# Counting the chosen memory rows once, from one-hot rows summed on GpSimd, in place of once per token tile on TensorE

## The reference

```python
qp = jnp.einsum('bld,ed->ble', q, Wq)
scores = jnp.einsum('bld,bmd->blm', qp, kv)
idx = jnp.argmax(scores, axis=-1)
mem = jnp.take_along_axis(kv, idx[..., None], axis=1)
mkv = jnp.einsum('bld,ed->ble', mem, Wkv)
mk, mv = jnp.split(mkv, 2, axis=-1)
logits = jnp.einsum('bhld,bmd->bhlm', qh, mk) * scale
attn = jax.nn.softmax(logits, axis=-1)
out = jnp.einsum('bhlm,bmd->bhld', attn, mv)
```

## Time and profile before

| | |
|---|---|
| Time, median of 3 runs | 1332.48 us (1331.79 to 1332.91) |
| Span of the profiled execution | 1333.5 us, 1.0 us above that median; no other time is given for it |
| PE busy | 1184.3 us (89%) |
| DVE busy | 975.1 us (73%) |
| ACT busy | 624.8 us (47%) |
| POOL busy | 182.8 us (14%) |
| Lookup stage | about 625.6 to 750 us |

### The profile page before, as it was taken

One profiled execution on the slowest core, in us unless ns is written; L12 is line 12 of the kernel. 1 busy time (PEld: TensorE's weight loads), 2 busy tenths in 40 slices (PEclk: granted clock), 3 DMA queues, 4 the chain that ended last, 5 costly groups with the idle time before them and its releaser, 6 DMA issues. The chain is left out here.

```text
span 1333.5 us, 18190 instructions
## 1 busy us (share of the span) xinstructions
PE 1184.3 (89%) x6745; PEld 633.7 (48%) x6745; DVE 975.1 (73%) x2195; ACT 624.8 (47%) x838; POOL 182.8 (14%) x165
## 2 busy tenths in 40 slices
PE   7994899999999999974999389999986799999997
PEld 3541223333333333243788112333334489899997
DVE  3564999898899988046799489999918466767675
ACT  1220245756756666741443015666653334444442
POOL 2223111021021100143000430500004000000000
PEclk9995799999999999986999559999987899999999
DMA  7215167920000000030110593200011000000000
GB/s 257 72 59 113 25 69 80 113 27 1 2 1 1 1 1 2 1 133 27 48 48 1 57 99 42 89 2 2 1 45 61 1 1 1 17 1 16 1 17 17
DMA packets 44760, 51.72 MB, mean 39 GB/s; under 512 B 7322, under 2 KB 40090, under 8 KB 44666
## 3 DMA queue, kind: packets, MB, share of 16 engines
q1 hardware_dynamic: 44666, 50.50, 19.7%
HBM read 38.36 MB, written 11.53 MB: 37 GB/s over the span
## 5 line engine op out<-in xcount | busy, mean ns | idle before, releaser
L572 ACT ACTIVATE self_probs<-self_scores 128x1024 f32<-128x1024 f32 (+3 forms) x320 | 273.3, 894 | 197.2 <-PE self_scores L526 195.9
L600 DVE TENSOR_REDUCE self_piece_max<-self_max 128x1 f32<-128x512 f32 x384 | 249.7, 685 | 22.9 <-PE self_max L511 21.4
L511 PE MATMUL self_max<-stack_k,stack_q 96*128 96x512 bf16 (+3 forms) x640 | 209.1, 367 | 21.2 <-DVE self_piece_max L600 9.0
L600 DVE TENSOR_REDUCE cross_piece_max<-cross_max 128x1 f32<-128x512 f32 x256 | 160.7, 683 | 25.6 <-PE cross_max L511 25.0
L572 ACT ACTIVATE cross_probs<-cross_scores 128x1024 f32<-128x1024 f32 x128 | 124.6, 1021 | 109.3 <-PE cross_scores L526 109.3
L526 PE MATMUL self_scores<-stack_q,stack_k 98*128 98x512 bf16 (+3 forms) x640 | 170.5, 350 | 4.3 <-DMA stack_q<-self_shift 3.0
L511 PEld LDWEIGHTS self_max<-stack_k,stack_q 96*128 96x128 bf16 x640 | 61.7, 97 | 201.8 <-DVE self_piece_max L600 102.5
L537 PE MATMUL self_out<-self_probs,V 128*17 128x512 f32 (+3 forms) x1280 | 148.8, 537 | 2.4 <-ACT self_probs L572 2.1
L596 DVE CUSTOM_DVE_ANT_0 self_junk<-self_max,causal_sb 128x128 bf16<-128x128 f32 (+3 forms) x256 | 120.8, 484 | 21.0 <-PE self_max L511 19.5
L1259 ACT ACTIVATE o_tok<-ph 128x512 f32<-128x512 f32 x96 | 57.5, 599 | 143.6 <-PE ph L92 137.4
L92 PE MATMUL py<-w_first,hid_first 128*128 128x256 f32 x384 | 108.7, 283 | 5.8 <-DVE x_sb L1321 5.8
(11 more groups left out here) (207 smaller groups left out, 1799.1 us busy)
## 6 DMA issues: line engine op xcount, KB each, us to landing
stack_q<-qparts SPq DMA_DIRECT2D x96, 64.0 KB, 8.9
stackx<-xparts SPq DMA_DIRECT2D x24, 256.0 KB, 11.1
stack_k<-kparts SPq DMA_DIRECT2D x18, 256.0 KB, 14.3
qparts<-parts SPq DMA_DIRECT2D x8, 384.0 KB, 2.5
kparts<-parts SPq DMA_DIRECT2D x8, 384.0 KB, 2.5
xparts<-xparts_sb SPq DMA_DIRECT2D x8, 384.0 KB, 2.8
cross_raw<-in_w SPq DMA_DIRECT2D x4, 768.0 KB, 4.4
n_raw<-in_w SPq DMA_DIRECT2D x6, 512.0 KB, 4.2
```

Source lines behind the costliest of these rows:

```text
L511: mm = nc.tensor.matmul(slot[:, 0:pc["w"]], pc["lhsT"], pc["rhs"], start=True, stop=True)
L572: nc.scalar.activation(probs[:, i % 3, 2 * pair:2 * pair + 2, st["off"]:C], ps[:, 2 * pair:2 * pair + 2, st["off"]:C], ACT.Exp, scale=SCAL ...
L600: ins = nc.vector.tensor_reduce(to, slot[:, 0:pc["w"]], AX.X, ALU.max)
```

## The change

The 13 matmuls for each tile go, and with them a matmul that cleared `pc`. In their place GpSimd adds each tile's one-hot rows to a sum `hits`, in place, 16 additions over 1601 elements of bf16. After the last of them PE multiplies `hits` with the column of ones, 13 matmuls once. `chosen` has 1601 columns for each buffer where it had 1664, and `hits` has 1664 and is cleared at the stage's start in place of `chosen`.

```diff
-                    chosen = sb(inner, "chosen", [P, 2, MP], BF16)
+                    chosen = sb(inner, "chosen", [P, 2, M], BF16)
+                    hits = sb(inner, "hits", [P, MP], BF16)
...
-                            nc.gpsimd.memset(chosen[:], 0.0).then_inc(set2, 1)
+                            nc.gpsimd.memset(hits[:], 0.0).then_inc(set2, 1)
...
+                            pool.wait_ge(set2, 3)
+                            for n in range(NT):
+                                pool.wait_ge(chosen_ready, n + 1)
+                                if n:
+                                    pool.wait_ge(counted, n)
+                                nc.gpsimd.tensor_tensor(hits[:, 0:M], hits[:, 0:M], chosen[:, n % 2], ALU.add).then_inc(counted, 1)
...
-                            def tally(n):
-
-                                pe.wait_ge(chosen_ready, n + 1)
-                                for t in range(MT):
-                                    mm = nc.tensor.matmul(pc[:, t:t + 1], chosen[:, n % 2, t * P:(t + 1) * P], ones_b[:, 0:1],
-                                                          start=False, stop=(n == NT - 1 and t == MT - 1), skip_group_check=True)
-                                mm.then_inc(counted, 1)
-
                             pe.wait_ge(set2, 6)
-                            nc.tensor.matmul(pc[:, 0:MT], zeros_b[:, 0:P], zeros_b[:, 0:MT], start=True, stop=False, skip_group_check=True)
...
-                                if n >= 2:
-                                    tally(n - 2)
-                            tally(NT - 2)
-                            tally(NT - 1)
+                            pe.wait_ge(counted, NT)
+                            for t in range(MT):
+                                mm = nc.tensor.matmul(pc[:, t:t + 1], hits[:, t * P:(t + 1) * P], ones_b[:, 0:1], start=True, stop=True)
+                            mm.then_inc(counted, 1)
...
-                                nc.vector.tensor_scalar(chosen[:, n % 2, 0:M], iota_sb[:], place_f[:, n % 2], None,
+                                nc.vector.tensor_scalar(chosen[:, n % 2], iota_sb[:], place_f[:, n % 2], None,
                                                         ALU.is_equal).then_inc(chosen_ready, 1)
...
-                            dve.wait_ge(counted, NT)
+                            dve.wait_ge(counted, NT + 1)
```

## The result

| | before | changed |
|---|---|---|
| Median of 20 runs each | 1333.05 us (1331.79 to 1335.63) | 1335.51 us (1332.48 to 1338.00) |
| Ratio, 95% interval | | 1.0015 (1.0009 to 1.0021) |
| Span of the profiled execution | 1333.5 us | 1335.6 us |
| First MAX8 to the counts read (L1086, now L1085) | 94.17 us | 95.08 us |
| First MAX8 to the next stage's first DMA | 104.77 us | 106.18 us |

The account below looks back on a forecast made before the run. PE was taken to bound the later tiles by a little, DVE right behind; 3.06 us gained in the loop, 3.94 lost at its end, the rest nothing: 1332.5 + 0.9 = 1333.4 us, range 1331.5 to 1338.0 for 8 in 10.

Parts of the forecast that it names:

- The loop gain: Tile loop without 14 tallies of 0.34 us on PE: MAX8 of tile 15 at 729.73, 3.06 us earlier.
- The halved clearing: GpSimd's clearing at the stage's start, 1664 for 3328 elements: nothing gained, since a DMA wait covers it.
- The addition A: GpSimd's addition of 1601 elements per tile: 3.06 us, with 1.6, 3.59 and 4.59 kept as ends.
- The hold: A DVE one-hot row stands still while a GpSimd addition runs and ends 0.80 us after it.
- The threshold: Inside the loop, additions start to cost through held one-hot rows from A = 3.85 us.
- The counts: DVE's read of the counts after the loop: 740.33 against 739.45 before, 0.9 us slower.
- the step on the clock: PE idles from about 730 to 740; should its clock rise later than before, a few tenths are lost.
- PE's lead: Tiles 2, 3, 4, 7 and 8 are set by DVE, or DVE and ACT; their tallies are hidden.
- The odd one-hot rows: Rival: rows in the second `chosen` buffer take 1.83 us for 1.06; 5.5 us slower, 1338.0; chance 8%.
- The additions did not outlast a tile: Rival that they do: at A = 4.59 pace 5.44, 12 us slower, 1344.6; 3.85 to 4.59 costs 3 to 12; 8%.
- A DVE that isn't held: Rival, loop end: without hold 0.1 us slower; or, with additions of 1.6 us, 1.4 faster, 1331.1; chance 14%.
- The loop did not gain more: Rival that it does: tiles set by DVE come out earlier, counts 1.7 us earlier with it all; 3%.

Follow-up runs that it names:

- the repeat of before: The kernel before run once more, nothing changed: ratio 0.9996 (0.9985 to 1.0007) to the kernel before.
- the filled kernel: Changed kernel plus three matmuls of zeros on PE behind the scores of tiles 3 and 7: ratio 1.0022 (1.0012 to 1.0032) to the kernel before.
- the repeat of the changed kernel: The changed kernel run once more, nothing altered: ratio 1.0010 (0.9997 to 1.0023) to the kernel before.

## Why the prediction was right, and where it was short

**The loop gain** was right in its size and its places: 3.06 us forecast, 3.15 measured. That 4.8 us of PE work gave only that was DVE's doing, at tiles 5, 6, 9 and 10, as worked out. Leaving the additions out changed nothing (91.00 against 91.01), so it is the tallies' gain alone. The halved clearing gave nothing, as forecast: it took 1.49 us for 2.88, and GpSimd's wait for the DMA behind it grew from 1.10 to 2.48.

**The addition A** was taken as 3.06 us from the row of 1602 elements. It is 3.25 at a multiple of 4 bytes and 2.94 off it; the two that matter are 3.21 and 2.93, in sum 6.14 for the 6.12 of the forecast. The trace of before also had 1024 elements at 2.37 us, where the forecast's line of 0.27 us and 1.75 ns an element gives 2.06; with the 1536 at 3.45 that made two rows against the line. That the sum fits so well is luck, since the forecast knew nothing of the two lengths: with both buffers aligned it was 3.21 + 3.20 = 6.41, and the counts came 0.28 us later. Still, the row nearest in size was the right choice; the 3.59 scaled from 1536 elements was not, nor the 3.52 us estimated from the Trainium skill ("GPSIMD Engine Reference", section 3.1).

**The hold** was right: the last one-hot row stood still till 0.85 us before its end (0.80 forecast), shown by taking the last two additions away (1.06), by putting back that of tile 14 alone (2.12) and by adding all to the kernel before (2.12). The threshold was forecast at 3.85 us, where A + 0.85 reaches DVE's 4.70; 4.8 us additions gave the pace A + 0.93, with 0.08 us from the row's end to the next addition, so it lies nearer 3.77, if the 0.93 holds there too; no run has additions between 3.3 and 4.7 us. Short additions kept off it in every tile but the last, where FIND_INDEX8 alone stands between two one-hot rows.

**The counts** came 0.91 us later, for 0.9 forecast; the repeat of before (94.16) and the filled kernel (95.05) give the same, the repeat of the changed kernel (96.65) does not.

**What fell short is the step on the clock.** The forecast had "should it rise later than before, a few tenths are lost", and put 1333.4 us. Measured was 2.0 us over before for 0.9, and 0.9 lies outside the interval of the first 20 runs (1.2 to 2.8), though not of the repeat (up to 3.1, down to -0.4). Two things stand over the 0.9. From the counts to the next stage's first DMA it took 10.60 us before, 11.10 in the changed kernel's first profile, with the transposes at half clock, and 10.77 in its second, where they took 0.65: 0.50 or 0.17 us. And the forecast held that the tallies of tiles 2 to 4 were hidden "by PE's lead" and so cost nothing to take away. They cost no path time, but they kept PE's idle time ahead of tile 4 at 0.8 us; without them it is 1.4 to 1.5, and in two of the nine profiles with that gap the clock fell to 0.50 there, with 1.6 us lost by the end of the loop (in none of the four with 0.8, and not in the one with long additions, whose gap was 2.6). Two falls in nine profiles against none in four are too few to show that the longer gap is the cause. As an estimate, two of nine times 1.56 is 0.35 us in the mean, and with 0.17 to 0.50 behind the counts it makes 1.4 to 1.8 in all. Whether that is the whole of the 2.0 stays open; the runs of one kernel spread over 4 to 10 us, and the profiles can't weigh how often each happens.

**The rivals.** The odd one-hot rows did not lose their pace: 1.05 us, and 1.06 in the even ones. The additions did not outlast a tile, but the kernel with long ones shows that this rival was priced about right (its pace A + 0.93 against A + 0.85). A DVE that isn't held is excluded. The loop did not gain more than worked out.

## What to carry to other kernels

Work that an idle engine takes over from the bound one is free only while something follows that hides it. The last unit is not hidden: here it cost 2.98 us, and the one before it 1.09 through the hold. Let the helper take all units but the last ones: 14 of 16 on GpSimd gave 3.16 us at the counts, where 16 of 16 lost 0.91. And before GpSimd is put to work, look in the trace for DVE operations from SBUF to SBUF that will meet it, however small, and whether they are of a kind that is held.

## What the runs showed of the hardware

- A GpSimd addition held two DVE operations that compare one SBUF input and write SBUF (TENSOR_SCALAR) to its end: 1601 elements 2.11 us for 1.06, and 13 elements 2.43 for 0.17. Not every DVE operation on SBUF is held: FIND_INDEX8 (1.82) and a cast of one element a partition (0.15) ran beside it at their usual length, and so did two that read PSUM (0.17 and 0.16).
- A GpSimd addition of bf16 was shorter when one operand started 2 bytes off a multiple of 4: 2.94 for 3.25 us, and 3.20 to 3.26 for all when both buffers were aligned.
- After 1.4 to 1.5 us of idle time PE's clock fell from 1.00 to 0.50 for about 3 us in one of two profiles of the changed kernel and in one of seven of its variants with the same gap. What decides it isn't shown.
